# V taken up right behind the second aggregation of a graph-and-transformer kernel

## What is computed

```python
x = x + gat2(relu(gat1(layernorm(x))))          # dense attention over the nodes' neighbours, bias after each
x = x + ffn(layernorm(x))[0]
# ffn: x = x + attention(layernorm(x, g1, b1)); x = x + moe(layernorm(x, g2, b2))
# attention: 12 heads of 64, qkv = x @ Wqkv, softmax, @ Wproj;  moe: 8 experts, top 2, 384 hidden
```

## Time and profile before

| | |
|---|---|
| median of 3 runs | 1751.6 us (1751.39 to 1755.18) |
| profiled execution, its own time | 1743.26 us |
| its span, first to last instruction | 1741.2 us |
| TensorE, VectorE, ScalarE, GpSimd busy | 84%, 67%, 55%, 29% |
| mean granted TensorE clock | 0.934 of full |

### The profile page before, as it was taken

One profiled execution on the slowest core, in us unless ns is written; L12 is line 12 of the kernel. 1 busy time (PEld: TensorE's weight loads), 2 busy tenths in 40 slices (PEclk: granted clock), 3 DMA queues, 4 the chain that ended last, 5 costly groups with the idle time before them and its releaser, 6 DMA issues.

```text
span 1741.2 us, 25808 instructions
## 1 busy us (share of the span) xinstructions
PE 1464.5 (84%) x8977; PEld 1366.2 (78%) x8977; DVE 1172.4 (67%) x1753; ACT 963.6 (55%) x1616; POOL 504.8 (29%) x379
## 2 busy tenths in 40 slices
PE   3996899995998397589889898898988898499986
PEld 1894689995988397378788787887878898499986
DVE  5798897356777410484876848858488577688774
ACT  7887884223653221064646646557467621388774
POOL 1000000000022323053434524545256510255433
PEclk9998899997999698689999999999999999699998
DMA  6001002211123511000000000000000297389864
GB/s 177 1 1 36 1 22 69 74 61 36 39 95 106 187 53 37 0 19 1 1 18 0 18 0 0 18 0 0 15 3 28 62 262 188 129 223 249 235 204 122
DMA packets 56018, 121.41 MB, mean 70 GB/s; under 512 B 7264, under 2 KB 23268, under 8 KB 55936
## 3 DMA queue, kind: packets, MB, share of 16 engines
q1 hardware_dynamic: 48448, 98.09, 17.8%
q0 software_dynamic: 7488, 22.26, 6.0%
HBM read 89.57 MB, written 33.70 MB: 71 GB/s over the span
## 4 chain that ended last, share of the span: by engine, by line
PE 29%; DVE 15%; DMA 12%; issue 7%; POOL 2%; ACT 2%; DVEq 0%; SPq 0%; POOLq 0%; ACTq 0%
DMA out_dram<-yrow,index 10%; DVE mcol L953 5%; PE ps L356 5%; PE ps L357 5%; PE ps L358 5%; DVE rz L962 4%; PE ps L755 3%; DVE prlo L923 2%; PE ps L775 2%; PE ps L794 2%; PE ps L777 2%; PE ps L796 2%; PE ps L795 2%; POOL prlo L923 1%; PE ps L764 1%
## 5 line engine op out<-in xcount | busy, mean ns | idle before, releaser
L923 POOL TENSOR_TENSOR prlo<-prob,prhi 125x500 fp32r<-125x500 f32 x180 | 255.7, 1426 | 370.8 <-ACT prob L887 370.7
L885 ACT ACTIVATE prhi<-ps 125x500 fp32r<-125x500 f32 x300 | 177.1, 590 | 122.2 <-PE ps L777 113.0
L953 DVE TENSOR_REDUCE mcol<-ps 125x1 f32<-125x1250 f32 x120 | 174.4, 1453 | 32.3 <-PE ps L755 31.6
L794 PE MATMUL ps<-prhi,vhi 125*128 125x250 f32 x600 | 172.8, 288 | 25.3 <-POOL prlo L923 12.9
L923 DVE TENSOR_TENSOR prlo<-prob,prhi 125x500 fp32r<-125x500 f32 x120 | 121.4, 1012 | 92.8 <-ACT prob L887 91.3
L887 ACT ACTIVATE prob<-ps 125x500 f32<-125x500 f32 x300 | 176.4, 588 | 3.1 <-DVE prlo L923 3.0
L1299 POOL TENSOR_TENSOR xnb<-xnb,lnrow 125x768 f32<-125x768 f32 x10 | 18.3, 1834 | 538.6 <-ACT xnb L1693 538.6
L796 PE MATMUL ps<-prlo,vhi 125*128 125x250 f32 x600 | 169.2, 282 | 0.0
L795 PE MATMUL ps<-prhi,vlo 125*64 125x250 f32 x600 | 168.4, 281 | 0.0
L775 PE MATMUL ps<-qst,kst 128*125 128x250 f32 x600 | 157.8, 286 | 4.7 <-ACT q L877 3.9
L1478 PE MATMUL ps<-ohs,ohd 128*125 128x417 bf16 x380 | 124.7, 391 | 39.1 <-DVE ohs L1933 38.5
(11 more groups left out here) (298 smaller groups left out, 4087.5 us busy)
## 6 DMA issues: line engine op xcount, KB each, us to landing
w2st<-in_L_ffn_W_dram SPq DMA_DIRECT2D x27, 1152.0 KB, 6.0
w1all<-in_L_ffn_W_dram SPq DMA_DIRECT2D x8, 1152.0 KB, 9.7
wqst<-in_L_ffn_Wqkv_dram SPq DMA_DIRECT2D x12, 384.0 KB, 4.0
hid_d<-tin SPq DMA_DIRECT2D x10, 375.0 KB
hin<-hid_d SPq DMA_DIRECT2D x10, 375.0 KB
vtin<-xn_d SPq DMA_DIRECT2D x10, 375.0 KB
out_dram<-accr POOLq DMA_DIRECT2D x10, 375.0 KB, 9.0
xall<-in_x_dram SPq DMA_DIRECT2D x5, 672.0 KB
```

What stands on the lines that cost most here:

```text
L794: pe.matmul(ps[:, b:b + GQ], vhi[:, e, kt, :], hi, start=kt == 0, stop=False)
L885: act.activation(prhi[:, n % RING, :], bank(3 + n % 3, P, 2 * GQ), ACT.Exp, scale=float(HD) ** -0.5)
L923: eng.tensor_tensor(prlo[:, n % RING, :], prob[:, n % 3, :], prhi[:, n % RING, :].bitcast(f32), ALU.subtract)\
L953: dve.tensor_reduce(mcol[:, e, t:t + 1], ps[0:P, 0:N], AX.X, ALU.max, negate=True).then_inc(sem("max"), 1)
```

## The change

- In the aggregation one set of moments serves both layer norms. The variance of `xa` follows from the variance v of `x1`, so DVE writes v + eps and v(1 + eps) + eps^2, and one root, one reciprocal and one product give scale and shift of both rows. The root of tile t is taken in the step after its moments, before `higher`. ACT writes `xa` and the normed row from the same `xres`, into one buffer each.
- The bias is added to the residual in place ahead of the sum's arrival (`before2`), and `finish2` is one operation on PSUM and the moments.
- Gain and bias move from POOL to DVE and to V: the row is stored without them, `v_in` loads it back, `v_affine` applies them in `vtin`.
- The V weights are loaded at the start of the aggregation and split in its steps (`ahead` on ACT, `after2` on DVE).
- The drains and waits at both borders of V are gone. `v_turn(0)` stands between the last two `sums`. The other nine `v_turn` alternate with nine half products `v_half` ahead of `project(0)`; one half stands behind it, and the other ten one behind each `rough(0, 0, t)`. The split writes straight into `xthi` and `xtlo`, without POOL's copies. `load_qk(0)` is issued as soon as all rows are stored.
- ACT waits once for its own `esb` writes in the first layer.

```diff
         def agg_pe(pe, n):
             sums(T - 2, 0)
+            v_turn(pe, 0)
             sums(T - 1, 1)
...
+        def v_turn(pe, t):
+            u = t % 2
+            if t == 0:
+                pe.wait_ge(sem("agg_lo"), 2 * T + 1)
+            else:
+                pe.wait_ge(sem("tile_lo"), 2 * T + t + 2)
+            pe.wait_ge(sem("v_row"), t + 1)
+            for k in range(KD):
+                at = k // 3 * BANK + k % 3 * P
+                last = pe.transpose(ps[:, at:at + P], vtin[:, u, k * 128:(k + 1) * 128], ident[0:P, 0:P])
+            last.then_inc(sem("tile_raw"), 1)
+        def v_half(pe, t, h):
+            if t == h == 0:
+                pe.wait_ge(sem("w_lo"), 3 * KD)
+            if h == 0:
+                pe.wait_ge(sem("tile_lo"), 2 * T + t + 3)
+                if t < 2:
+                    pe.wait_ge(sem("agg_read"), 2 * T + t + 1)
+                else:
+                    pe.wait_ge(sem("tile_yfree"), 2 * T + t + 1)
+            for k in range(KD):
+                last = three(pe, bank(4 + 2 * u + h, P, HALF), xthi[:, k, t * P:(t + 1) * P], xtlo[:, k, t * P:(t + 1) * P],
+                             wvhi[:, k, h * HALF:(h + 1) * HALF], wvlo[:, k, h * HALF:(h + 1) * HALF], k == 0, k == KD - 1)
+            if h == 1:
+                last.then_inc(sem("tile_y"), 1)
+        def v_affine(dve, t):
+            u = t % 2
+            if t == 0:
+                dve.wait_ge(sem("lnrow_in"), 32)
+            dve.wait_ge(sem(f"tile_in{u}"), 16 * (T // 2 + t // 2 + 1))
+            dve.tensor_tensor(vtin[:, u, :], vtin[:, u, :], lnrow[:, 0, :], ALU.mult).then_inc(sem("v_scaled"), 1)
+            dve.wait_ge(sem("v_scaled"), t + 1)
+            dve.tensor_tensor(vtin[:, u, :], vtin[:, u, :], lnrow[:, 1, :], ALU.add).then_inc(sem("v_row"), 1)
...
+        def agg_act(act, n, root, rows, after):
...
                 if k + 1 < T:
                     exponential(act, n, k + 1)
+                root(k)
                 if k < T:
                     higher(act, n, k)
                 if k + 2 < T:
                     sloped(act, n, k + 2)
+                rows(k)
                 if k + 4 < T:
                     distant(act, n, k + 4)
+                after(k)
...
+            def rows2(k):
+                t = k - 3
+                if 0 <= t < T:
+                    act.wait_ge(sem("rstd_a"), t + 1)
+                    for n, buf, c in (("xa", xab, 4), ("xn", xnb, 5)):
+                        if t >= 1:
+                            act.wait_ge(sem(f"{n}_out"), 32 * t)
+                        act.activation(buf[:, :], xres[:, t % 2, :], ACT.Identity, scale=stat[:, t % 2, c:c + 1],
+                                       bias=stat[:, t % 2, c + 2:c + 3]).then_inc(sem(f"{n}_row"), 1)
...
+            def after2(k):
+                if 0 <= k - 3 < KD:
+                    dve.wait_ge(sem("w_hi"), KD * 2 + k - 2)
+                    dve.tensor_tensor(wvlo[:, k - 3, :], wvst[:, k - 3, :], wvhi[:, k - 3, :].bitcast(f32),
+                                      ALU.subtract).then_inc(sem("w_lo"), 1)
+                if k in (T - 2, T - 1):
+                    v_affine(dve, k - (T - 2))
+                if k == T:
+                    v_lower(dve, 0)
+                    v_affine(dve, 2)
+                if k == T + 1:
+                    v_lower(dve, 1)
+            agg_dve(dve, order, 1, before2, finish2, after2)
+            for t in range(2, T):
+                if t + 1 < T:
+                    v_affine(dve, t + 1)
+                v_lower(dve, t)
...
         def attention_pe(pe):
+            for i in range(T - 2):
+                v_turn(pe, i + 1)
+                v_half(pe, i // 2, i % 2)
+            v_turn(pe, T - 1)
+            v_half(pe, T // 2 - 1, 0)
+            pe.wait_ge(sem("tile_lo"), 3 * T + 2)
             project(0)
+            v_half(pe, T // 2 - 1, 1)
             for t in range(T):
                 rough(0, 0, t)
+                v_half(pe, (T + t) // 2, t % 2)
             maxima(0, 0)
+            pe.wait_ge(sem("tile_yfree"), 3 * T + 2)
             start(0, 0)
...
+            def g2_rows(t):
+                for n, dram, buf in (("x1", out, xres[:, t % 2, :]), ("xa", xa_d, xab[:, :]), ("xn", xn_d, xnb[:, :])):
+                    sp.wait_ge(sem(f"{n}_row"), t + 1)
...
+                if t + 2 < T:
+                    sp.wait_ge(sem("x1_out"), 32 * (t + 1))
+                    x_in(t + 2)
+            def v_in(t):
+                if t >= 2:
+                    sp.wait_ge(sem("tile_raw"), 2 * T + t + 1)
+                sp.wait_ge(sem("xn_out"), 32 * (t + 1))
+                sp.dma_start(vtin[:, t % 2, :], xn_d[t * P:(t + 1) * P, :]).then_inc(sem(f"tile_in{t % 2}"), 16)
...
+            for t in range(T - 2):
+                g2_rows(t)
+                if t == 3:
+                    v_in(0)
+                    v_in(1)
+            v_in(2)
+            g2_rows(T - 2)
+            v_in(3)
+            v_in(4)
+            g2_rows(T - 1)
+            v_in(5)
+            for n in ("x1", "xa", "xn"):
+                sp.wait_ge(sem(f"{n}_out"), 32 * T)
             load_qk(0)
+            for t in range(6, T):
+                v_in(t)
...
+            pool.wait_ge(sem("agg_sum"), 2 * T + 2)
+            order.did(pool.memset(q2[:, :, :].bitcast(f32), 0.0))
             split_qk(0)
+            pool.wait_ge(sem("v_row"), T)
             order.did(pool.memset(k2[:, :, :].bitcast(f32), 0.0))
+            pool.wait_ge(sem("tile_y"), 3 * T + 2)
+            order.did(pool.memset(vhi[:, :, :, HD:].bitcast(f32), 1.0))
+            pool.wait_ge(sem("tile_yfree"), 3 * T + 2)
             set_v(0, 0, 0)
             set_v(0, 0, 1)
```

More of the change, by code:

```diff
@@ L207, in build @@
     xres = put("xres", [P, 2, D], f32, at=W2AT)
-    xab = put("xab", [P, 2, D], f32, at=put.end)
-    xnb = put("xnb", [P, 2, D], f32, at=put.end)
-    lnrow = put("lnrow", [P, 2, D], f32, at=put.end)
+    xab = put("xab", [P, D], f32, at=put.end)
+    xnb = put("xnb", [P, D], f32, at=put.end)
+    wvhi = put("wvhi", [128, KD, D], f32r, at=put.end)
+    WVAT = put.end
+    wvst = put("wvst", [128, KD, D], f32, at=WVAT)
+    wvlo = put("wvlo", [128, KD, D], f32r, at=WVAT)
+    vtin = put("vtin", [P, 2, D], f32, at=put.end)
+    lnrow = put("lnrow", [P, 2, D], f32, at=ATT)
     GRAPH_TOP = top[0]
@@ L377, in split_pool @@
                     .then_inc(sem("w_lo"), 1)
[L383 to L415, removed]
@@ L428, in ring_sp @@
[L428 to L433, removed]
         def transposes2(pe, t):
@@ L688, in agg_dve @@
             dve.wait_ge(sem("agg_w"), T * n + 1)
-            agg_steps(step)
+            for k in range(T + 3):
+                step(k)
             dve.wait_ge(sem("agg_w"), T * (n + 1))
@@ L907, in attention_act @@
             act.sem_inc(sem("exp"), 3)
-            split_qk(0)
+            for t in range(T // 2 - 1):
+                v_higher(act, 2 * t + 2)
+                v_higher(act, 2 * t + 3)
+                v_out(act, t)
+                if t == 1:
+                    split_qk(0)
             set_raw(0)
             set_k(0, 0)
+            v_out(act, T // 2 - 1)
             set_q(0, 0)
+            for t in range(T // 2, T):
+                v_out(act, t)
             set_m(0, 0)
@@ new lines, in ahead @@
+            def ahead(k):
+                if k == 2:
+                    for m in range(2):
+                        act.wait_ge(sem(f"w_in{m}"), 16 * (KD // 2 * 3))
+                if 0 <= k - 2 < KD:
+                    act.activation(wvhi[:, k - 2, :], wvst[:, k - 2, :], ACT.Copy).then_inc(sem("w_hi"), 1)
+                if k == T:
+                    v_higher(act, 0)
+                if k == T + 1:
+                    v_higher(act, 1)
+            broadcast_act(act, 1)
+            agg_act(act, 1, root, rows2, ahead)
@@ L2041, in inverse @@
                 order.wait()
[L2042 to L2043 removed]
+                alone(dve)
+                if t >= 2:
+                    dve.wait_ge(sem("xn_row"), t - 1)
+                order.did(dve.bn_aggr(stat[:, u, 0:2], bn[:, u, :]))
+                order.wait()
+                dve.tensor_scalar(stat[:, u, 2:3], stat[:, u, 1:2], EPS, None, ALU.add)
```

239 lines of the change are left out of this document (63 added, 176 removed).

## The result

The changed kernel takes 1670.9 us (median of 4 runs, 1667.0 to 1673.7), the kernel before beside it 1752.5 us. The ratio is 0.955, 95% interval 0.952 to 0.958: 4.5% faster. The profiled execution took 1673.7 us with a span of 1672.0.

What follows compares the result with a forecast made beforehand. TensorE was held to waiting: a cross-engine loop pacing late aggregation at 15.9 us steps, borders around V, and rough tiles at about half clock. Gains less stalls sum to 84.8 us, from 1751.6 to 1666.8 us, range 1655 to 1688.

Steps and rivals of the forecast that it cites:

- Aggregation, 15.8 us: Second aggregation's last five tiles: cutting the cross-engine loop brings steps from 15.9 to 11.63 us, gaining 15.8 us.
- Border into V, 31.9: Between last sums and V: norms, affine, weights' load and split and a store no longer hold TensorE, gaining 31.9 us.
- V itself, 2.3: V's product: ten tiles at full clock take 69.0 us against 71.3, gaining 2.3 us.
- Stalls ahead of the product, minus 4: V's turns before the first Q and K product: late turns, late loads and one DVE-POOL meeting cost 4 us.
- the ring turn, issue, landing, affine with two buffers: V's row loads: with 4.4 us landing, 7.4 us for two turns, 3.7 per turn, just under 3.8.
- the memsets: Memsets, with the first layer's `esb` wait: cost nothing, as their engines idle there.
- The meeting of `v_affine` and POOL's split, 1.7 us once: In V, DVE's affine may meet POOL's Q and K split: 1.7 us once, up to 3.43 by the skill's rule.
- Border behind V, 11.0: Between V and the first product: Q and K weights' load and splits lie under half products, gaining 11.0 us.
- First product, 2.9: First Q and K product: 21.1 us at full clock instead of 24.0 at 0.88, gaining 2.9 us.
- Rough tiles, 24.9: First product to first scores: V's halves cover split and reductions, 36.2 us becomes 11.3, gaining 24.9 us.
- The aggregation's loop: Rival: aggregation keeps a cross-engine loop or DVE is the bound, 13.5 us steps, 9 us back, 1676; chance 0.10.
- The way through DRAM paces V: Rival: V's row loads land near 9.4 us and pace its turns, 19 us back, 1686; chance 0.12.

Runs made afterwards that it cites:

- Reads alone: Two GpSimd operations per second-layer tile on SBUF rows nobody needs, added to the changed kernel: 1678.2 us, ratio 0.960.
- cut loads: Each load of a tile's rows into V split into transfers of 112 and 13 rows, against the changed kernel: 1665.4 us, again 1668.8.
- six places: Six places instead of two for loaded rows in V, transfers keeping their shape, against the changed kernel: 1666.1 us, ratio 0.953.
- changed again: The changed kernel measured a second time, nothing altered: 1676.2 us, ratio 0.958 to the kernel before.
- halves first: All 20 halves of V's product put ahead of the first projection, rough tiles alone behind it, against the changed kernel: 1700.5 us, ratio 0.972.
- Q and K late: First head pair's Q and K weights loaded behind V's last turn, split by ACT behind tile 3's output, against the changed kernel: 1678.6 us.

## Why the prediction was right, and where it was not

**Aggregation, 15.8 us: right, 16.3.** Steps of 11.63 us to the end. The loop was cut as described; norms put back into the step bring 8.2 us of it back. The prediction held the slowed `weigh` for a part of it. Reads alone cost no step at all and hit another instruction; 4.1 us more come back when the loop is there too. The last 4.0 are open.

**Border into V, 31.9, and V itself, 2.3: right.** V without waits took 34.6 us for the nine turns with a half that I had at 34.2. The second tile's turn ran at 551.02, directly behind the sums. That the border's 31.9 us went with all its parts at once is seen; only the 7 us of V's early start were tried alone.

**Stalls ahead of the product, minus 4: the term that was mis-sized.** The idle time is 12.3 us, and with the slower clock (0.97) and slower turns the stretch is 11.2 longer than forecast. The mechanism was named in the prediction, the ring turn, issue, landing, affine with two buffers, and so was the rival in which it paces V. The failing step is "with 4.4 us landing that is 7.4 us for two turns": the row it was taken from is a load of weights in 128 rows, this one is 125 rows in one transfer and lands after 5.1 to 7.0 us. The bound that I set aside, 9.4 us, was too high, the value taken too low; by 6.2 us the ring gives (0.6 + 0.3 + 6.2 + 2.1)/2 = 4.6 per turn and 6 us of wait, and TensorE's waits ahead of `v_turn` 5, 6, 7 and 9 are 6.6. The other 5.7 stand ahead of `v_turn(2)` and `v_turn(3)`, 2.4 and 3.3 where the prediction had 0.2 and 0.5, and come from what queues around the last rows' stores. Cutting the load or adding places gives 10.4 or 7.4 us back, in part by way of the second wait below. That I had the loads of tiles 4 to 6 at one or two turns late by 1 us was too little as well. Two waits I hadn't listed. The first: `v_affine(2)` stands on DVE ahead of the reciprocal of tile 8, and its load came 4.01 us late; `xab` of that tile then started after 8.92 us of idle time on ACT:

```profile
549.18 0.96 DVE L514 TENSOR_TENSOR vtin<-vtin,lnrow 125x768 f32<-125x768 f32 x1 [4.01 <-DMA vtin<-xn_d]
...
553.49 1.03 ACT L1670 ACTIVATE xab<-xres,stat 125x768 f32<-125x768 f32 x1 [8.92 <-DVE stat L2027]
```

The second lies between these two rows. The prediction put "the memsets" at nothing because their engine is idle. GpSimd's `memset` of `q2` starts when the last sums end, and DVE's operation of line 2027, which `xab` waits for, runs beside it for 2.21 us instead of 0.23 (rows in the last section). So about 2.0 us of this chain are the memset's; `v_turn(2)`, whose split stands behind DVE's reading of the last sum, is late in part by it too. With cut loads and with six places the operation comes early enough and takes 0.23 us. Moving the memset alone was not tried.

**The meeting of `v_affine` and POOL's split, 1.7 us once: right, 1.6.** It happened at 581.73:

```profile
579.53 3.92 POOL L1317 TENSOR_TENSOR wqlo<-wqst,wqhi 128x1536 fp32r<-128x1536 f32 x1 [26.10 <-ACT wqhi L855]
...
581.73 2.54 DVE L514 TENSOR_TENSOR vtin<-vtin,lnrow 125x768 f32<-125x768 f32 x1 [0.77 <-DMA vtin<-xn_d]
```

It takes 2.54 us and ends 0.82 us after POOL's instruction. The Trainium skill's rule that was weighed in the prediction (SBUF — State Buffer, Who interferes with whom) is borne out: DVE was locked out until POOL was done, and the price was 1.6 only because it came 2.2 us late to a lock of 3.92. With cut loads it came 0.8 us behind the split's start (573.98 and 573.19) and took 3.50 us, a price of 2.5, which is nearer to the bound that the prediction worked out by the rule.

**Border behind V, 11.0: right.** No wait is left ahead of the product, and 6.4 come back when loading and splitting are late; a part stays covered there.

**First product, 2.9: right.** 24.4 us with a half, forecast 24.3.

**Rough tiles, 24.9: right, and 3 us too careful.** The tiles are 3.76 us apart, forecast 4.0; a rough tile takes 0.73 us, not 0.83, and from `maxima` to the first scores it takes 2.6 us, not 3.0. Undoing this one edit costs 28.4.

**The rivals.** The aggregation's loop didn't stay, the halves hide, the clock stays up. "The way through DRAM paces V" was half true: the mechanism decides the stretch, at 8 us over the 4 assumed instead of 19. The errors of 11.2 and 3.2 us left 8.5 behind the last sums. In the profiled executions the span is 15.6 us above the forecast's 1656.4: 8.0 in distance, 7.1 in the unchanged code behind the first scores, 0.5 ahead. Between the medians only 3.9 us are left, since the profiled execution of before was 8.3 us under its median and that of after 2.8 above. That is luck and no merit of the working: the stretches that the change touches gained 76.8 us, not 84.8.

## What to carry to other kernels

A load's landing time is read from a row of the same shape: the number of rows can decide how many DMA engines are busy with it, and a cut into 112 and 13 of 125 rows gave 10 us in a ring where four more buffers, the obvious try, gave 7. An engine's slack in a step hides contention only for that step's own deadline; ask who else is fed from behind the slowed instruction. An idle engine's work isn't free either if it can hold up another engine's next instruction. When TensorE and DVE take turns on small tiles, other products between them are worth more than their sum, since they keep the clock up too.

## What the runs showed of the hardware

- A transfer of 125 rows of 3 KB kept 0.32 of 16 DMA engines busy at 118 GB/s and landed 5.1 to 7.0 us after its issue; in 112 and 13 rows it kept 0.66 busy at 186 GB/s and landed after 4.1 to 5.0.
- A VectorE instruction with two SBUF inputs that started behind a GpSimd instruction reading SBUF ended 0.8 us after that one in the three cases looked at, and took 2.60, 2.54 and 3.50 us instead of 0.95. When VectorE's was first, GpSimd's was the longer one: 3.00 us against 1.84 behind `leaky`, which began 0.20 us earlier and kept its 1.51 (kernel with GpSimd's reads, 493.10 and 504.03), and 3.92 for the split at 579.53 (3.43 in the kernel before), behind a sum of `v_affine` that began at 579.15 and kept its 0.96.
- A VectorE scalar operation on two elements per row (0.23 us elsewhere) that met a GpSimd `memset`, which reads nothing, ended with it, and so did the sum of two rows behind it. In the three other profiled executions where the two met (changed again, halves first, Q and K late) it took 2.29, 1.88 and 1.85 us and ended 0.02 to 0.03 us after the memset. Operations of VectorE that read PSUM or took statistics beside the memset kept their 1.02 us (cut loads, 552.34 and 553.60):

```profile
551.24 2.19 POOL L1344 MEMSET q<- 128x2500 f32 x1 [540.50 <-PE ps L357]
551.24 2.21 DVE L2027 TENSOR_SCALAR stat<-stat 125x2 f32<-125x2 f32 x1
551.38 2.07 DVE L2032 TENSOR_TENSOR xres<-xres,brow 125x768 f32<-125x768 f32 x1
```

- Unchanged code behind the first scores took from 1000.0 to 1015.8 us in 14 profiled executions, so single executions tell nothing about a change of 1%.
